# Fourth layer's shift rows: one ScalarE copy of the turned maxima, two GpSimd broadcasts

## The reference

```
v = (values @ Wv.T).reshape(N, Lv, 16, 8)
k = (keys @ Wk.T).reshape(N, Lk, 16, 8)
q = (query @ Wq.T).reshape(N, Lq, 16, 8)
energy = einsum('nqhd,nkhd->nhqk', q, k)
attn = softmax(energy / sqrt(128), axis=3)
out = einsum('nhql,nlhd->nqhd', attn, v).reshape(N, Lq, 128) @ Wo.T + bo
```

## Time and profile before

| | |
|---|---|
| median of 3 runs | 856.37 us (855.8 to 856.83) |
| the profiled execution's own time | 857.73 us |
| its span, from first to last instruction | 855.9 us |
| mean granted TensorE clock over the span | 0.938 of full speed |
| busy: TensorE, VectorE, ScalarE, GpSimd | 754.6, 609.3, 418.5, 329.4 us |
| the attention stage around the change | about 609 to 759 us of the span |

### The profile page before, as it was taken

One profiled execution on the slowest core, in us unless ns is written; L12 is line 12 of the kernel. 1 busy time (PEld: TensorE's weight loads), 2 busy tenths in 40 slices (PEclk: granted clock), 3 DMA queues, 4 the chain that ended last, 5 costly groups with the idle time before them and its releaser, 6 DMA issues.

```text
span 855.9 us, 15688 instructions
## 1 busy us (share of the span) xinstructions
PE 754.6 (88%) x5632; PEld 496.1 (58%) x5632; DVE 609.3 (71%) x1264; ACT 418.5 (49%) x682; POOL 329.4 (38%) x255
## 2 busy tenths in 40 slices
PE   4599999996777979987899999997898998988997
PEld 3577777786445576653455555563246665654675
DVE  4789999998886665566555666568788997515653
ACT  2476666673465624424444545411047776734331
POOL 0665555553523602550677777721160100000111
PEclk9799999997888958999999999998869999899999
DMA  7256766432425530205023332026834767000220
GB/s 202 81 196 215 245 207 201 160 121 83 60 84 180 160 99 8 85 30 161 1 75 89 118 92 75 0 34 100 115 97 101 121 145 148 3 2 25 92 93 23
DMA packets 50583, 88.35 MB, mean 103 GB/s; under 512 B 17375, under 2 KB 34975, under 8 KB 50167
## 3 DMA queue, kind: packets, MB, share of 16 engines
q1 hardware_dynamic: 50518, 87.49, 38.1%
HBM read 61.97 MB, written 25.51 MB: 102 GB/s over the span
## 4 chain that ended last, share of the span: by engine, by line
PE 46%; DVE 37%; ACT 5%; issue 5%; POOL 4%; DMA 2%; SPq 0%; DVEq 0%; POOLq 0%; ACTq 0%
DVE arena L2341 8%; PE ps L1109 8%; DVE arena L1740 8%; PE ps L1099 6%; DVE rn L1895 4%; PE ps L1277 3%; DVE arena L1944 3%; PE ps L1042 3%; PE ps L1214 3%; PE ps L1287 3%; DVE arena L1923 2%; PE ps L1203 2%; DVE arena L1903 2%; POOL arena L1694 2%; ACT arena L1538 2%
## 5 line engine op out<-in xcount | busy, mean ns | idle before, releaser
L2341 DVE TENSOR_REDUCE arena<-ps 112x1 f32<-112x500 f32 x192 | 114.9, 669 | 15.9 <-PE ps L1186 15.8
L1740 DVE TENSOR_TENSOR arena<-ps,arena 128x448 f32<-128x448 f32 (+7 forms) x138 | 83.4, 629 | 58.4 <-ACT arena L1562 19.7
L1694 POOL TENSOR_TENSOR arena<-arena 125x448 f32<-125x448 f32 x96 | 109.5, 1141 | 24.2 <-ACT arena L1507 21.2
L1109 PE MATMUL ps<-arena 125*128 125x448 f32 (+1 forms) x208 | 97.1, 548 | 1.4 <-ACT arena L1507 0.9
L1538 ACT ACTIVATE arena<-ps 125x896 f32<-125x896 f32 x96 | 87.0, 917 | 21.8 <-PE ps L1203 21.6
L1507 ACT ACTIVATE arena<-arena,kbias 125x448 f32<-125x448 f32 x96 | 63.7, 668 | 65.3 <-DVE arena L1740 46.3
L1740 DVE TENSOR_TENSOR arena<-ps,rn 125x448 f32<-125x448 f32 x96 | 59.3, 618 | 47.7 <-PE ps L1099 43.3
L1099 PE MATMUL ps<-arena 128*125 128x448 f16 (+3 forms) x312 | 77.9, 360 | 3.0 <-DVEq L1751 3.0
L1099 PEld LDWEIGHTS ps<-arena 128*125 128x125 f16 (+1 forms) x312 | 40.9, 135 | 57.2 <-issue 42.3
L801 PE MATMUL ps<-w_k2h,arena 128*125 128x512 f16 x288 | 67.9, 388 | 6.8 <-ACT arena L1343 5.2
L1671 POOL TENSOR_TENSOR arena<-arena 112x512 f32<-112x512 f32 x24 | 30.4, 1267 | 89.5 <-DVE arena L1740 89.4
(11 more groups left out here) (305 smaller groups left out, 1496.1 us busy)
## 6 DMA issues: line engine op xcount, KB each, us to landing
arena<-in_ctxT SPq DMA_DIRECT2D x8, 750.0 KB, 8.1
d_cln<-arena SPq DMA_DIRECT2D x8, 750.0 KB
d_clnT<-arena SPq DMA_DIRECT2D x8, 750.0 KB
d_k<-arena SPq DMA_DIRECT2D x24, 250.0 KB
d_v<-arena SPq DMA_DIRECT2D x24, 250.0 KB
arena<-d_clnT SPq DMA_DIRECT2D x8, 750.0 KB
arena<-in_ctx SPq DMA_DIRECT2D x8, 672.0 KB
arena<-d_cln SPq DMA_DIRECT2D x8, 672.0 KB
```

What stands on the lines that cost most here:

```text
L1109: pe.matmul(ps[0:D, 4 + 2 * p, 0:N], cln_s[p][0:rows, t, :], pexp[(t + p) % 2][0:rows], start=(t == 0), stop=(t == KT)).then_inc(l2_pv, 1)
L1694: ins = pool.tensor_tensor(psum2[p][0:rows], psum2[p][0:rows], pexp[(t + p) % 2][0:rows], ALU.add)
L1740: return dve.tensor_tensor(out, a, b, op)
L2341: dve.tensor_reduce(mx3[bn % 2][:, u % 2, u % 8 // 2, u // 8:u // 8 + 1], ps[0:TT, max_bank_of(bn, u), 0:500], AX.X, ALU.max).then_inc(l3_ ...
```

## The change

A tile `turned3` of 68 x 112 in fp16 is added. ScalarE now copies partitions 0 to 67 of the transposed bank into it with one instruction (`copy_maxima3`), at the place where its two casts stood, and signals `l3_tn`. The `max_sim` that follows in the rotation waits for `l3_tn` instead of `l3_row`. GpSimd makes the two broadcast rows of `qst3` from `turned3`, with a wait for its own first one before the second and for both at the end; `sim3` still waits for `l3_row`. For b > 0 the ScalarE copy waits until GpSimd has read the previous one. A one-element Exp is put ahead of the first copy. GpSimd's order becomes: masks 1 to 3, shift rows of batch 0, spread 0, mask 4, spread 1, masks 5 to 7, and then shift rows of b and spread of b + 1 in alternation.

```
--- before.py
+++ after.py
@@ -389,6 +389,7 @@
         m3 = carve([TT, 2, 64])
         sm8 = carve([TT, 8, NT, 8])
         wt3 = carve([TT, NT, 8])
+        turned3 = carve([68, TT], F16)
         at[0] = core_end
         h3 = [carve([D, 4, N]) for _ in range(2)]
         wh3 = [carve([D, 2, 2 * FF], F16) for _ in range(2)]
@@ -468,6 +469,7 @@
         l3_ldv = [sem(f"l3_values_loaded{i}") for i in range(2)]
         l3_pad = sem("l3_pad_loaded")
         l3_v = sem("l3_values_spread")
+        l3_tn = sem("l3_turned_maxima_copied")
         l3_q = sem("l3_queries_ready")
         l3_mx = [sem(f"l3_max_sim{r}") for r in range(2)]
         l3_mxd = sem("l3_max_done")
@@ -1170,7 +1172,7 @@
                 if at >= 3:
                     b_was, u_was = MAX_ORDER[at - 3]
                     if u_was == TURN:
-                        pe.wait_ge(l3_row, 2 * (b_was + 1))
+                        pe.wait_ge(l3_tn, b_was + 1)
                     else:
                         pe.wait_ge(l3_mxd, 24 * b_was + u_was + 1)
                 return MAX_BANKS[at % 3]
@@ -1517,18 +1519,18 @@
             act.wait_ge(l3_q, 1)
             act.copy(q3, ps[0:D, 0:4, 0:N]).then_inc(l3_free, 1)
 
-            def shift_rows3(b):
+            def copy_maxima3(b):
                 act.wait_ge(l3_sh, b + 1)
-                for r, heads in ((0, slice(0, 2)), (64, slice(2, 4))):
-                    act.copy(qst3[r:r + 4, b:b + 1, :, heads, :].rearrange("p o g h q -> p (o g) (h q)"),
-                             ps[r:r + 4, max_bank_of(b, TURN), 0:TT].unsqueeze(1).broadcast_to([4, 4, TT]))\
-                        .then_inc(l3_row, 1)
+                if b:
+                    act.wait_ge(l3_row, 2 * b)
+                act.copy(turned3, ps[0:68, max_bank_of(b, TURN), 0:TT]).then_inc(l3_tn, 1)
 
             def outputs3(b):
                 act.wait_ge(l3_pv, KT * (b + 1) + 2)
                 act.copy(o3[:, b].rearrange("p h q -> p (h q)"), ps[0:D, 6, 0:224]).then_inc(l3_o, 1)
 
-            shift_rows3(0)
+            act.activation(exs[0][0:1, 0:1], tg[0:1, 0:1], ACT.Exp)
+            copy_maxima3(0)
             for b in range(B):
                 for t in range(KT):
                     n = KT * b + t
@@ -1540,7 +1542,7 @@
                     if t == 0 and b:
                         outputs3(b - 1)
                     if t == KT - 3 and b + 1 < B:
-                        shift_rows3(b + 1)
+                        copy_maxima3(b + 1)
             outputs3(B - 1)
 
 
@@ -1715,14 +1717,31 @@
                                          v3c[p][:, :, 96:D].rearrange("p j (g c) -> p j g c", c=HD16)))
                 pool.nop().then_inc(l3_v, 1)
 
+            def shift_rows3(b):
+
+                pool.wait_ge(l3_q, B if b else 4)
+                pool.wait_ge(l3_tn, b + 1)
+                for r, heads in ((0, slice(0, 2)), (64, slice(2, 4))):
+                    if r:
+                        pool.wait_ge(l3_row, 2 * b + 1)
+                    pool.tensor_copy(qst3[r:r + 4, b:b + 1, :, heads, :].rearrange("p o g h q -> p (o g) (h q)"),
+                                     turned3[r:r + 4].unsqueeze(1).broadcast_to([4, 4, TT])).then_inc(l3_row, 1)
+                pool.wait_ge(l3_row, 2 * b + 2)
+
             pool.wait_ge(l3_free, 2)
             pool.wait_ge(l3_q, 1)
+            for b in range(1, 4):
+                query_masks(pool, b, q3[:, :, S * b:S * b + S])
+            shift_rows3(0)
+            spread_values3(0)
+            query_masks(pool, 4, q3[:, :, 4 * S:5 * S])
+            spread_values3(1)
+            for b in range(5, B):
+                query_masks(pool, b, q3[:, :, S * b:S * b + S])
             for b in range(1, B):
-                query_masks(pool, b, q3[:, :, S * b:S * b + S])
-                if b < 3:
-                    spread_values3(b - 1)
-            for b in range(2, B):
-                spread_values3(b)
+                shift_rows3(b)
+                if b + 1 < B:
+                    spread_values3(b + 1)
 
             rsqrt()
             ch.link(pool.memset(y2, 0.0))
```

## The result

The changed kernel takes 848.40 us, median of ten runs (842.92 to 852.9), beside 856.62 us before (ten runs, 855.4 to 868.63). The ratio is 0.9888, 95% interval [0.9862, 0.9914], that is 9.6 us less, 7.4 to 11.8. The ratio leaves out the one run of 868.63 us, which was in the chip's slower state. I had forecast 850.8 us, 5.6 less, within 847 to 854.5. The profiled execution has a span of 847.5 us against 855.9.

A forecast was written before the change was run, and what follows sets the result against it. VectorE's 24 maxima pace a batch, with 0.91 us lost per turn to ScalarE's casts; gains 1.35 + 3.28 + 0 + 0.17 + 0.82 = 5.62 us give 850.8 us, range 847 to 854.5.

The forecast's parts named there:

- ScalarE, two casts to one copy, and turns 1 to 4: At turns between batches, Exp and pv3 come 0.82 us sooner, ending most of VectorE's idle; four turns, 3.28 us.
- GpSimd's pair: Two broadcast copies at each turn, 0.56 us each, 1.46 us from ScalarE's copy to the rows, hidden by pv3 of tile 10.
- the forecast 0.05 us of cover: At a turn, the rows are ready at 646.45, 0.05 us before sim3 wants them; each us beyond delays VectorE one for one.
- The rule of 2.6 cycles per element: Skill page on GpSimd's elementwise work: a copy would be 0.97 us plus dispatch, losing most of the turn's gain; not followed.
- The bank released earlier: max_sim waits for ScalarE's copy instead of the rows; in steady work it stands behind pv3 anyway: gains nothing.
- The start: Batch 0: table load moved ahead, the first Exp 1.40 us sooner, the first pv3 gains 1.35 us.
- the 1.55 us of "issue": ScalarE's idle between the first casts and the table load at the start; taken as a place to weigh the skill page.
- The drain of the Trainium skill's page: At the start, the page adds a drain to the 1.28 us table load, 2.66 in all; gain limited by the scores.
- The stall takes turn 5: TensorE stops near 722 us, taken as code fetched late behind loads issued at 708.99; the stall grows, turn 5 gains nothing.
- Turn 6 gains 0.17: Turn right after the stall, at low clock, where TensorE waited only 0.17 us for the Exp: gain 0.17 us.
- Turn 7: Last turn, maxima over, TensorE waits 1.19 us for the Exp: the full 0.82 us gained.
- The clock at the start: TensorE's low clock from 632 to 637 us may end up to two tiles earlier, another 1.5 us; outside the forecast sum.

The follow-up runs named there:

- e2: The changed kernel without the one-element Exp put ahead; 850.73 us, ratio 0.9906 to the kernel before.
- e5: The changed kernel with each of GpSimd's two broadcast copies made twice; 860.13 us, ratio 1.0041 to the kernel before.
- e6: The changed kernel, but the max_sim after the transposed bank waits again for both shift rows instead of ScalarE's copy; 847.65 us, ratio 0.9884 to the kernel before.
- e4: The kernel before with the first experts' weight loads held back until TensorE has passed four tiles of batch 6; 855.23 us, ratio 0.9963.
- e3: The changed kernel with the first experts' weight loads held back until TensorE has passed four tiles of batch 6; 846.54 us, ratio 0.9874 to the kernel before.
- e13: The same kernel as e3, run on another chip beside the changed kernel; 845.66 us, ratio 0.9877 to the kernel before.
- e1: The kernel before with only the one-element Exp put ahead of the first turn's casts; 858.52 us, ratio 1.0016.
- e11: The kernel before with the one-element Exp, experts' weights held back and five unread matmuls ahead of tile 10's pv3 at each turn; 856.05 us, ratio 0.9973.
- e10: The kernel before with the one-element Exp ahead and the experts' weight loads held back; 858.53 us, ratio 1.0004.
- e12: The changed kernel run again without any edit, beside others on one chip; 847.96 us, ratio 0.9897 to the kernel before.
- e9: The kernel before with the one-element Exp and five unread matmuls ahead of tile 10's pv3 at each turn; 857.12 us, ratio 1.0000.
- e7: The changed kernel with two unread matmuls (512 and 168 columns) behind each unit of batch 0's maxima; 861.40 us, ratio 1.0053 to the kernel before.

## Why the prediction was right, and where not

The range held and the direction; the sum was too small, 5.6 us forecast against 8.2 by the medians and 8.23 in the profiled stage. In the profile the 2.61 us between them are 0.80 of clock at the start, 0.43 at turns 1 to 4, 1.35 at turns 5 and 6 and 0.03 in the rest. The measured 848.40 lies 1.4 us above the lower end of the range; that it lies inside owes something to luck, because the largest of these terms stood nowhere in the forecast. By its own steps:

- *ScalarE, two casts to one copy, and turns 1 to 4*: right. Forecast 0.82 per turn, measured 15.82 - 14.89 = 0.93, because the Exp starts 0.15 us after the start of the copy and not behind its 0.25. 3.71 us against 3.28. e2 shows that the turns and not the load ahead carry the change.
- *GpSimd's pair*: the copies are 551 ns against 560 forecast. The pair starts at 641.91 and takes 1.16; `sim3` starts at 643.22, 0.58 behind its `pv3` where it was 0.52. In e5 `sim3` starts 0.15 after the last copy's end (660.47 + 0.55 = 661.02), and 643.07 + 0.15 is 643.22: the pair is the last to come, the forecast 0.05 us of cover is -0.06. From the copy's end (641.78) to `sim3` it is 1.44 us against 1.46 forecast, by errors that cancel: 0.06 between the two copies and not 0.18, but hand-overs of 0.13 and 0.15 and not 0.08 each. It costs so little only because it is so close. The rule of 2.6 cycles per element (the Trainium skill, GPSIMD Engine Reference, section 3.1) was not one for these copies: the same section lays it to the two inputs of its `tensor_tensor`, and a broadcast copy has one. The trace agrees that it does not hold here: 0.55 us for 448 elements.
- *The bank released earlier*: nothing, right (e6).
- *The start*: 1.28 us for the first Exp against 1.40, right. The old table load began at 628.59 as the scores' row ended (627.55 + 1.07 = 628.62), so the 1.55 us of "issue" ahead of it was, by these rows, a wait for the scores. The drain of the Trainium skill's page (ScalarE: Activation LUTs, "What ACT_TABLE_LOAD costs") is not seen in this gain, which is the load's own 1.28, and could not be told apart where the load now stands, because nobody waits there.
- *The stall takes turn 5*: in this pair of profiles, as forecast. Counted from "up", the stop begins 6.71 us sooner than before, which is the gain of the start and five turns (2.08 + 3.71 + 0.93), and ends 5.89 sooner: it is 0.82 longer, 3.12 against 2.30. But its length varies from run to run, and e4 against e3 and e13 does not show on the medians that it swallowed anything. What was shown is that the stall hangs on the experts' weights, issued from 713.96 on, and not on the keys of 708.99 alone, which e4 and e13 also load.
- *Turn 6 gains 0.17*: the term that was mis-sized most. Interval 7 is 2.11 us shorter. Without any low clock there, turn 6 is worth 14.67 (e1, e11) - 13.93 (e13) = 0.74. The other 1.37 is the low clock behind the stall, which the sum kept as it was: it made interval 7 longer by 16.47 - 14.67 = 1.80 us before and by 14.36 - 13.93 = 0.43 after, because it lasted about 6.8 us before and 3.4 after, and in the changed kernel began 2 us ahead of the turn's copy (granted clock 0.89 from 718 to 733, against 0.78 from 726 to 741). What sets its length, no run here shows. Intervals 6 and 7 together gained 1.52 us, where forecast were 0.17 and the two turns without a stall give 0.93 + 0.74.
- *Turn 7*: 0.82 forecast, 0.92 measured with what follows it.
- *The clock at the start*: left out of the sum, with up to 1.5 us in the range. In the profile it gave 2.08 - 1.28 = 0.80. It does not hang on the load ahead alone: interval 1 of e2, without it, is 0.78 shorter than before.

And a step that I did not have at all: behind ScalarE's two casts, where TensorE waits 0.89 us, its clock can fall, for 1.3 to 1.4 us each in e1 and e10, and behind turns 6 and 7 in e4. The two profiles of the old turns without the load ahead, before and e4, show none at turns 1 to 5, so the profile that I read could not tell it, and how often it happens in the kernel before is not shown. The change takes that wait away, and in all six profiles of kernels with the changed turns whose rows were not delayed (after, e2, e3, e6, e12, e13) no turn lost clock from 1 to 5. That the wait brings the fall is borne out by the fillers of e9 and e11; that it is not enough is shown by e5, and what else decides stays open. The mean granted clock over the runs is 0.944 for the changed kernel, 0.943 in e12 and 0.940 in e6, beside 0.939 and 0.938 for the kernel before on the chips of these two: a small difference, of one sign.

Upstream and downstream of the stage the two profiles differ by about a microsecond each way; nothing was changed there. What stays open is how the mean gain divides between the turns and the clock. In the one pair of profiles the start and seven turns are 1.28 + 5 x 0.93 + 0.74 + 0.92 = 7.6 us, the clock at the start 0.80, and the stall with the low clock behind it costs 0.15 more than before (18.57 - 14.89 + 0.43 = 4.11 against 17.98 - 15.82 + 1.80 = 3.96); together the 8.2 of the stage. Whether the 8.2 to 9.6 us of the medians and the ratio divide the same way, the intervals do not tell.

## What to carry to other kernels

At a hand-over inside a software pipeline, read how long each engine in the ring waits behind the slow step: a second engine's short wait costs its length, and TensorE's may cost its clock as well, which one profile can fail to show; look at more than one profile and at the mean clock of many runs. A single-instruction copy out of PSUM with the spreading done by an idle engine pays if the idle engine's time fits under work that must come first anyway; here it fits to within 0.1 us, and each further copy counts in full. Loads that nobody needs yet are better issued after a burst that others need: here this left at most 0.5 us of the stall, and took 3.2 us from the kernel before (e4); behind the change its gain is not secured.

## What the runs showed of the hardware that I had not expected

- The falls of the clock behind turns recurred: in e1 and e10, once turn 2 had lost clock, every later one up to the fifth did, and in e10, which has no stall, turns 6 and 7 too, at intervals of 17.2 us in place of 15.8. With 0.79 us of unread matmuls in the wait there were none (e9 up to turn 5, e11 throughout). In e5 waits of 1.2 us brought none at turns 1 to 5.
- A TensorE that the profile shows busy throughout can stay at 1.2 GHz: 24 us of it stand in e7's rows, in matmuls of 500, 512 and 168 columns in turn (the ends of matmuls are modelled in a profile, so "busy" can hide short gaps); the clock came back only after the tiles had begun.
- On ScalarE an Exp can start 0.15 us after a copy of 0.25 us starts; back to back they overlap by 0.10.
